# Tiles 2 and 3 of a grouped convolution in float32 by shared blocks and edges, with the turn of a tile issued last on VectorE

## The reference

```python
out = conv(x, weight, groups=4, taps=9, pad=4)          # x: (128, 32, 512)
y   = out + (c @ c_weight.T)[:, :, None] + bias[None, :, None]
base_out = y @ base_W.T + base_b                        # over the last axis, 512 -> 512
probs = softmax(y @ router_W.T + router_b)              # 15 routes
topk_p, topk_i = top_k(probs, 8)
w = sum over k of topk_p * onehot(expert_map[topk_i])   # 8 experts
lora = ((y @ A.T) * w) @ B * 2.0                        # 8 experts of rank 16
x + base_out + lora
```

## Time and profile before

| | us |
|---|---|
| median of 3 runs | 184.52 (184.43 to 621.96) |
| the profiled execution, its own time | 184.44 |
| its span in the profile | 182.6 |
| PE busy | 178.4 (98%), 1236 instructions |
| DVE, POOL, ACT busy | 150.8, 139.8, 81.2 |

### The profile page before, as it was taken

The page is one execution under the profiler, slowest core; times in us unless marked ns, Lnnn a source line. Parts: engine busy times, 40 slices in busy tenths (PEclk is TensorE's granted clock), DMA queues, the critical chain, the costliest instruction groups (busy, mean ns, idle before and its releaser), DMA issues.

```text
span 182.6 us, 3930 instructions
## 1 busy us (share of the span) xinstructions
PE 178.4 (98%) x1236; PEld 171.1 (94%) x1236; DVE 150.8 (83%) x509; ACT 81.2 (44%) x247; POOL 139.8 (77%) x139
## 2 busy tenths in 40 slices
PE   7999999999999999999999999999999999999993
PEld 3687999999999999999999999999999999999992
DVE  0597888898888889888888988889898889978673
ACT  3648743354544434454443445454344444422320
POOL 2118999999888898888889888888988887885620
PEclk9999999999999999999999999999999999999999
DMA  6999751757475553646565454656445721233304
GB/s 172 348 388 340 252 178 14 243 199 204 152 233 174 173 181 124 178 152 230 159 198 174 135 170 154 228 178 210 175 106 201 230 78 63 97 115 115 118 0 172
DMA packets 17876, 32.01 MB, mean 175 GB/s; under 512 B 1984, under 2 KB 3136, under 8 KB 17856
## 3 DMA queue, kind: packets, MB, share of 16 engines
q1 hardware_dynamic: 17424, 31.40, 53.1%
q10 hardware_dynamic: 432, 0.36, 0.6%
HBM read 23.36 MB, written 8.39 MB: 174 GB/s over the span
## 4 chain that ended last, share of the span: by engine, by line
PE 96%; DVE 2%; issue 0%; POOL 0%; DVEq 0%; POOLq 0%
PE wide_ps L606 62%; PE wide_ps L648 12%; PE conv_banks L592 11%; PE edge_bank L592 3%; PE conv_banks L606 2%; PE odd_bank L635 2%; PE wide_ps L554 2%; PE conv_banks L663 1%; PE conv_banks L565 1%; PE conv_banks L563 1%; DVE xr L966 1%; DVE y L856 0%; DVE y_rows L774 0%; PE edge_bank L621 0%; DVE y_hi L891 0%
## 5 line engine op out<-in xcount | busy, mean ns | idle before, releaser
L606 PE MATMUL wide_ps<-wide_hi,y_hi 128*128 128x400 f32 (+1 forms) x248 | 66.0, 326 | 0.1
L606 PE MATMUL wide_ps<-wide_hi,y_lo 128*128 128x400 f32 (+1 forms) x248 | 62.6, 313 | 0.0
L606 PE MATMUL wide_ps<-wide_lo,y_hi 128*128 128x400 f32 (+1 forms) x248 | 62.5, 313 | 0.0
L486 POOL TENSOR_TENSOR terms_lo<-terms,terms_hi 128x512 fp32r<-128x512 f32 x28 | 36.3, 1298 | 18.4 <-ACT terms_hi L385 18.4
L606 PEld LDWEIGHTS wide_ps<-wide_hi,y_hi 128*128 128x128 f32 x248 | 44.0, 188 | 2.5 <-issue 0.5
L606 PEld LDWEIGHTS wide_ps<-wide_lo,y_hi 128*128 128x128 f32 x248 | 45.9, 188 | 0.0
L606 PEld LDWEIGHTS wide_ps<-wide_hi,y_lo 128*128 128x128 f32 x248 | 45.9, 188 | 0.0
L504 POOL TENSOR_TENSOR y_lo<-y,y_hi 128x512 fp32r<-128x512 f32 x31 | 40.3, 1299 | 5.7 <-ACT y_hi L400 5.7
L481 POOL TENSOR_TENSOR xr<-xr,base_b_sb 128x512 f32<-128x512 f32 x32 | 41.7, 1302 | 0.0
L407 ACT ACTIVATE hw_hi<-odd_bank 128x128 fp32r<-128x128 f32 x31 | 8.6, 278 | 54.3 <-PE odd_bank L635 54.3
L768 DVE TENSOR_TENSOR xr<-wide_ps,xr 128x512 f32<-128x512 f32 x30 | 20.7, 691 | 5.2 <-PE wide_ps L648 3.8
(11 more groups left out here) (90 smaller groups left out, 308.4 us busy)
## 6 DMA issues: line engine op xcount, KB each, us to landing
xr<-x_rows SPq DMA_DIRECT2D x32, 256.0 KB, 3.6
out<-xr SPq DMA_DIRECT2D x31, 256.0 KB, 3.2
terms<-x_units SPq DMA_DIRECT2D x28, 256.0 KB, 2.9
edges<-x_edges SPq DMA_DIRECT2D x14, 256.0 KB, 3.1
wide_sb<-wide_w SPq DMA_DIRECT2D x4, 328.0 KB, 4.9
x_in<-x_first SPq DMA_DIRECT2D x3, 264.0 KB, 4.7
weights_sb<-conv_w SPq DMA_DIRECT2D x2, 192.0 KB, 5.3
x_in<-x_first SPq DMA_DIRECT2D x2, 132.0 KB, 2.8
```

Of the source, the lines that this page charges most:

```text
L486: nc.gpsimd.tensor_tensor(terms_lo[i % 2][:, :, :, :], terms[i][:, :, :, :], terms_hi[i % 2][:, :, :, :].bitcast(F32), ALU.subtract)\
L606: mm = nc.tensor.matmul(sums_of(t, k)[:, b, 0:columns[1] - columns[0]], a[k % 2][:, r, :], w[:, r, columns[0]:columns[1]], start=r == 0 an ...
```

## The change

Tiles 2 and 3 no longer load whole blocks into `x_in` but even and odd blocks apart (`first_terms`) and one tile of edges (`first_edges`). `conv_whole` multiplies them by the shared, own and edge weights in plain float32, 256 columns each: three products for tile 2, two for tile 3. The differences that they need are made by POOL (tile 2 and the edges) and by DVE (tile 3), from SBUF to SBUF. Two weight blocks less are loaded, the pieces are cut otherwise, and the piece with the shared sums and quarter (now piece 4) is loaded ahead of piece 3. ACT takes the conditions of groups 2 and 3 ahead of `conv_high(1)`. On DVE the third addition of a condition becomes a function of its own (`reach`), and in every step the order is: two additions of the condition, `hw_low`, `choose`, `best`, `reach`, `add_out`, `mark`, `difference`, `weigh`, and the turn at the end. ACT takes `hw_high` ahead of `y_high` up to step 29. On POOL `bias_rows(0)` stands ahead of `edge_low(2)`. PE's `conv` waits for the edge's bank only ahead of the edge's products. `last_steps` is unchanged.

```diff
@@ -47,19 +48,18 @@
-W_OWN, W_REACH = (1, 2, 5, 6), (0, 3, 4, 7)
-W_SUM, W_QUARTERS = (8, 9, 11, 12), (10, 13)
-W_ALL = 14
+W_OWN, W_REACH, W_SUM, W_QUARTERS = (1, 2, 4, 7), (0, 3), (9, 10, 5, 8), (11, 6)
+W_ALL = 12
 COND = N + C + GROUPS + 2 * ROUTES
 W_PIECES = (slice(COND, COND + 2 * P), slice(COND + 2 * P, COND + 4 * P),
-            slice(COND + 4 * P, COND + 8 * P), slice(COND + 8 * P, COND + 11 * P),
-            slice(COND + 11 * P, COND + 14 * P))
-S_OWN, S_SUM, S_QUARTERS, S_ALL = (0, 1, 5, 6), (2, 3, 7, 8), (4, 9), 10
-S_PIECES = ((slice(0, 2), slice(1, 3), (0, 1)), (slice(2, 5), slice(8, 11), (3,)),
-            (slice(5, 7), slice(5, 7), (2,)), (slice(7, 10), slice(11, 14), (4,)))
+            slice(COND + 4 * P, COND + 7 * P), slice(COND + 7 * P, COND + 9 * P),
+            slice(COND + 9 * P, COND + 12 * P))
+S_OWN, S_SUM, S_QUARTERS, S_ALL = (0, 1, 5, 8), (2, 3, 6, 9), (4, 7), 10
+S_PIECES = ((slice(0, 2), slice(1, 3), (0, 1)), (slice(2, 5), slice(9, 12), (4,)),
+            (slice(5, 8), slice(4, 7), (2,)), (slice(8, 10), slice(7, 9), (3,)))
 def build(nc, x_first, x_units, x_edges, x_rows, conv_w, wide_w, up_w, base_b, out):
...
@@ -101,11 +101,14 @@
-        x_in = [sb(f"x_in{i}", [P, Q, BLKI]) for i in range(START)]
+        x_in = [sb(f"x_in{i}", [P, Q, BLKI]) for i in range(FIRST)]
+        first_terms = [sb(f"first_terms{i}", [P, 2, Q, MK]) for i in range(START - FIRST)]
+        first_edges = sb("first_edges", [P, 2, Q, MK])
         terms = [sb(f"terms{i}", [P, 2, Q, MK]) for i in range(URING)]
...
@@ -281,10 +292,13 @@
             load_conv(2)
-            load_x(2)
+            load_first_terms(0)
             sync.wait_ge(wide_in[0], 16)
+            sync.dma_start(first_edges[:, :, :, :], x_edges[0]).then_inc(first_edges_in, 16)
+            load_conv(4)
+            sync.wait_ge(wide_in[1], 16)
             load_conv(3)
-            load_x(3)
+            load_first_terms(1)
             sync.wait_ge(wide_in[2], 16)
...
@@ -414,12 +427,12 @@
             bias_condition(range(1, 2), 2)
+            bias_condition(range(2, GROUPS), 3)
             conv_high(1)
...
             exponentials(0, 0)
-            bias_condition(range(2, GROUPS), 3)
             terms_high(START, 0)
...
@@ -431,11 +444,14 @@
                     return
-                if up_to_tile(t, TILES - 2):
+                if t == TILES - 2:
                     y_high(t + 1, k + 1)
...
                 hw_high(t - 1, k - 1)
+                if up_to_tile(t, TILES - 3):
+                    y_high(t + 1, k + 1)
                 if up_to_tile(t, TILES - 2):
...
@@ -512,6 +528,14 @@
             conv_low(0)
+            pool.wait_ge(first_terms_in[0], 16)
+            nc.gpsimd.tensor_tensor(first_terms[0][:, 0, :, :], first_terms[0][:, 0, :, :],
+                                    first_terms[0][:, 1, :, :], ALU.subtract)\
+                .then_inc(first_difference[0], 1)
+            pool.wait_ge(first_edges_in, 16)
+            nc.gpsimd.tensor_tensor(first_edges[:, 0, :, :], first_edges[:, 0, :, :],
+                                    first_edges[:, 1, :, :], ALU.subtract)\
+                .then_inc(first_edge_ready, 1)
             conv_low(1)
...
@@ -521,14 +545,14 @@
                     up_low()
-                    edge_low(p + 2, k // 2)
                     pool.wait_ge(base_b_in, 16)
                     bias_rows(t, k)
+                    edge_low(p + 2, k // 2)
                     y_low(t + 2, k + 2)
...
                 if t == 1:
+                    bias_rows(t, k)
                     terms_low(t + 4, k)
-                    bias_rows(t, k)
                     edge(p + 3, 1 - k // 2)
...
@@ -572,21 +596,15 @@
                          (conv_ps[:, h, 1, :, :], S_OWN[g], terms_hi[h][:, 0], terms_lo[h][:, 0])]
-                if t == START:
-                    pe.wait_ge(y_rows_ready, t - 1)
-                    pe.wait_ge(cond_biased, GROUPS)
-                elif h == 0:
-                    pe.wait_ge(y_rows_ready, t)
-                else:
-                    pe.wait_ge(y_rows_ready, t - 1)
+                pe.wait_ge(y_rows_ready, t - 1)
                 if h == 0:
...
                     if n == 2:
+                        pe.wait_ge(y_rows_ready, t)
                         pe.wait_ge(edge_lo_ready, p - START // 2 + 1)
...
@@ -669,11 +687,24 @@
             cond_sums(range(1, 2), 2)
-            def conv_later(t):
+            def conv_whole(t):
+                i, h = t - FIRST, t % 2
                 pe.wait_ge(y_rows_ready, t - 1)
-                pe.wait_ge(conv_w_in[2], 16)
-                pe.wait_ge(x_loaded[t], 16)
-                conv_first(t)
+                pe.wait_ge(conv_w_in[2 + i], 16)
+                pe.wait_ge(first_terms_in[i], 16)
+                nc.tensor.matmul(conv_ps[:, h, 0, :, :], conv_sb[:, W_SUM[t], :],
+                                 first_terms[i][:, 1, :, :], start=True, stop=True)
+                pe.wait_ge(first_difference[i], 1)
+                mm = nc.tensor.matmul(conv_ps[:, h, 1, :, :], conv_sb[:, W_OWN[t], :],
+                                      first_terms[i][:, 0, :, :], start=True, stop=True)
+                if h == 0:
+                    pe.wait_ge(cond_biased, GROUPS)
+                    pe.wait_ge(first_edge_ready, 1)
+                    mm = nc.tensor.matmul(edge_ps, conv_sb[:, W_QUARTERS[t // 2], :],
+                                          first_edges[:, 0, :, :], start=True, stop=True)
+                mm.then_inc(conv_done, 1)
             def first_step():
...
@@ -779,21 +810,26 @@
                 rows = y_rows[h]
-                reached = slice(EDGE, P) if h == 0 else slice(0, EDGE)
                 dve.wait_ge(conv_done, t + 1)
...
                     .then_inc(common_ready, 1)
-                dve.wait_ge(common_ready, t - START + 1)
+                dve.wait_ge(common_ready, t - FIRST + 1)
                 nc.vector.tensor_tensor(rows[:, :, other, :], conv_ps[:, h, 1, :, :],
                                         rows[:, :, shared, :], ALU.add).then_inc(own_ready, 1)
-                dve.wait_ge(own_ready, t - START + 1)
+            def reach(t, g):
+                h = g % 2
+                shared = 1 - h
+                rows = y_rows[h]
+                reached = slice(EDGE, P) if h == 0 else slice(0, EDGE)
+                dve.wait_ge(own_ready, t - FIRST + 1)
                 nc.vector.tensor_tensor(rows[reached, :, shared, :], edge_ps[reached],
...
@@ -898,36 +934,40 @@
             best(0, 0)
-            difference(START, 0)
             dve.wait_ge(top_ready, 1)
             mark(0, 0)
+            dve.wait_ge(first_terms_in[1], 16)
+            nc.vector.tensor_tensor(first_terms[1][:, 0, :, :], first_terms[1][:, 0, :, :],
+                                    first_terms[1][:, 1, :, :], ALU.subtract)\
+                .then_inc(first_difference[1], 1)
+            difference(START, 0)
             dve.wait_ge(is_expert_ready, 1)
...
                 if t == 0:
-                    condition_first(2)
+                    condition(2, 2, 0)
+                    reach(2, 2)
                     turn(2, 2)
+                    hw_low(0, 0)
                     choose(1, 1)
...
                     best(1, 1)
+                    condition(3, 3, 0)
+                    reach(3, 3)
+                    return
+                if t == 1:
+                    add_out(0, 0)
                     dve.wait_ge(top_ready, 2)
                     mark(1, 1)
-                    condition_first(3)
-                    hw_low(0, 0)
-                    return
-                if t == 1:
+                    difference(START + 1, 1)
+                    weigh(1, 1)
                     turn(3, 3)
-                    difference(START + 1, 1)
-                    add_out(0, 0)
-                    weigh(1, 1)
                     return
...
                     condition(t + 2, (k + 2) % GROUPS, q + (k + 2) // GROUPS)
-                    turn(t + 2, k + 2)
-                    hw_low(t - 1, k - 1)
-                elif t == TILES - 2:
+                if up_to_tile(t, TILES - 2):
                     hw_low(t - 1, k - 1)
...
@@ -943,17 +983,19 @@
                     return
-                if up_to_tile(t, TILES - 2):
-                    choose(t, k)
-                    dve.wait_ge(logits_ready, t + 1)
-                    if up_to_tile(t, TILES - 5):
-                        difference(t + 4, k)
-                    best(t, k)
-                    dve.wait_ge(top_ready, t + 1)
-                    if up_to_tile(t, TILES - 3):
-                        add_out(t - 1, (k - 1) % UNROLL)
-                    mark(t, k)
-                    weigh(t, k)
+                choose(t, k)
+                dve.wait_ge(logits_ready, t + 1)
+                best(t, k)
+                if up_to_tile(t, TILES - 3):
+                    reach(t + 2, (k + 2) % GROUPS)
+                    add_out(t - 1, (k - 1) % UNROLL)
```

(7 more changed lines are left out.)

29 lines of the change are left out of this document (18 added, 11 removed).

## The result

The changed kernel takes 186.88 us (median of 6 executions, 186.31 to 188.23) beside 184.83 us for the kernel before on the same chip: a ratio of 1.0126 with a 95% interval of 1.0076 to 1.0176, so 2.3 us slower (1.4 to 3.3). That is within 2%, as forecast, and slower by more than the 0.9 us forecast, outside the range of 184.5 to 186.3.

What follows compares the result with a forecast made beforehand. PE bounds the kernel, with 96% of the chain of waits. From a span of 182.6 us, less 0.6 at the start, 0 in the middle, plus 1.6 at the end, plus 1.8 around it: 185.4 us, range 184.5 to 186.3.

Steps and rivals of the forecast that it cites:

- Cost: none, with 1.4 us of cover: Start: POOL's two subtractions of 0.75 us fit where POOL stood idle, before PE asks for the edges; no cost.
- 0 us, 28 times over: Middle steps: the new order moves operations later, but covers of 0.75 to about 1 us absorb it; 0 us.
- Tail, +1.6: Last steps: the late turn of tile 31 delays `y_hi`, `y_lo` and PE's front bank; 1.6 us lost, bounds 1.4 to 1.8.
- The rival that hides it: Tail: idle time absorbs the last turn's delay, so only the start counts; 183.8 or 183.1 us, chance 0.08.
- gains 0.6 us: Start: 1.29 us of PE work removed, 0.4 given back waiting for `up_lo` and 0.2 for `edge_lo`; 0.6 us gained.
- the sense of the rival: Middle: PE's transpose waits for `odd_up` behind the later `difference`; 188.2 us and more, slower by over 2%, chance 0.04.
- The rival of DVE and POOL blocking each other: Start: POOL's subtractions and DVE's two-input SBUF operations wait for each other; 0.5 to 0.8 us on the sum, chance 0.25.
- the pair at 14 us: Start: DVE's subtraction for tile 3 beside POOL's `conv_lo`, colliding for 0.4 us of POOL's full queue if the engines block.
- The base: Whole kernel: counted from the profiled execution of 184.44 us, span 182.6 and 1.8 around it; median taken as 184.52.
- 1.29 us less work: Start, PE: tile 2's convolution costs 0.43 us less and tile 3's 0.86 less, 1.29 us of work removed.

Runs made afterwards that it cites:

- before_tail_late: Kernel before with only step 29 in the changed order (turn of tile 31 last, `y_high` behind `hw_high`): 186.78 us, 1.0094.
- after_4: Changed kernel run again unedited for one more trace; the traced execution took 186.64 us.
- after_3: Changed kernel run again unedited for one more trace; the traced execution took 187.37 us.
- after_2: Changed kernel run again unedited, a second set of 6 executions: 186.96 us, 1.0113; the traced execution took 187.90 us.
- after: First profiled execution of the changed kernel, unedited: 188.23 us, where that set's median is 186.88 us.
- no_up_lo: tail_mid with POOL's subtraction for the low part of the up weights left out, zeros in its place: 184.73 us, 1.0000.
- pool_reads: Kernel before plus two POOL subtractions, SBUF to a scratch tile, placed beside DVE's `wide_lo`: 186.06 us, 1.0054.
- sub_late: Changed kernel, but POOL's first subtractions wait until DVE has made all four `wide_lo`: 186.86 us, 1.0108.
- sub_late_2: sub_late run once more, on the same chip as after_2: 186.39 us, 1.0086.
- both_mended: Changed kernel with the edit of sub_late and step 29 in the old order on DVE and ACT: 185.54 us, 1.0028.
- tail_mid: Changed kernel with sub_late's edit; in step 29 DVE turns right behind `reach`, `add_out` goes last, ACT takes `y_high` ahead of `hw_high`: 185.17 us, 1.0028.
- old_middle: Changed kernel with sub_late's edit, and DVE and ACT in the old order from step 2 to the end: 185.71 us, 1.0045.
- no_subs: tail_mid with the three subtractions for tiles 2 and 3 replaced by one-element fills: 184.71 us, 0.9989.

## Why the prediction was wrong

Two terms that the prediction put at nothing cost time: POOL's two subtractions beside `wide_lo` ("Cost: none, with 1.4 us of cover"), which cost 0.3 to 1.2 us, and the middle ("0 us, 28 times over"), which cost 0.5.

- **Tail, +1.6.** Right: 1.58 to 1.60 in the four traces of the changed kernel, and 1.63 in `before_tail_late`, which has nothing else of the change. The path was the one written down. The rival that hides it is dead.
- **The start, "gains 0.6 us".** This step failed, by the collision. Its four pieces, by PE's starts (the forecast is worked out from the prediction's own terms):

  | us | before | forecast | after_4 | after_3 | after_2 | after |
  |---|---|---|---|---|---|---|
  | cond sums to the next products | 0.36 | 0.36 | 0.69 | 1.03 | 1.57 | 1.57 |
  | tile 2's convolution to tile 3's | 3.91 | 3.58 | 3.66 | 3.66 | 3.67 | 3.67 |
  | tile 3's to transpose 0 | 1.72 | 0.86 | 0.86 | 0.87 | 0.86 | 0.86 |
  | transposes 0 to 1 | 5.50 | 6.07 | 6.12 | 6.15 | 6.14 | 6.13 |

  Left out is the piece between the first two, 0.68 before and 0.70 or 0.71 after. The last three pieces are within 0.1 of the forecast each and give a gain of 0.4 to 0.5. `no_up_lo` shows that the wait between the transposes is `up_lo`'s, with `edge_lo` behind it. The first piece takes 0.33 of that back in `after_4`, and more than all of it (0.67 to 1.21) in the others. The prediction asked who would wait for POOL's subtractions, and was right that nobody does; it didn't put into the sum that they hold up DVE's `wide_lo`, for which PE waits. `pool_reads` shows that cause alone. With the edit of `sub_late` and the whole computation the start still takes 11.87 to 12.19 (`sub_late`, `sub_late_2`, `both_mended`, `tail_mid`, `old_middle`), a gain of 0 to 0.3, since there the collision at `y_lo` of tile 1 takes about 0.3.
- **The middle, "0 us, 28 times over".** This step failed: +0.46 to +0.56 in each of the four traces of the changed kernel. 0.14 of it is the one late start of `hw_hi` of tile 24, 0.3 the slower odd step; the cause of both stays open. No cover was gone in the sense of the rival: each distance is within 0.3 of before.
- **The rival of DVE and POOL blocking each other**, at 0.25, is what happens in every trace of the changed kernel, and I had priced it at 0.5 to 0.8 on the sum. It is 0.3, 0.7 or 1.2 by the execution. Of its two places only the first collides there; the pair at 14 us costs there 0.06 of DVE's time at most, and more only behind the edit of `sub_late`. Over both sets the changed kernel's 14 executions have a mean of 187.1, the 12 of `sub_late` one of 186.7: 0.4 on the mean, 0.2 on the median, what the collision costs less what that edit costs. I had weighed the rival by what the rows of before could show. They could show nothing, since in that trace DVE's two-input operations never met POOL at work. Where a change brings two engines together for the first time, that silence is no evidence against. In another execution of the old start they do meet: in `before_tail_late` `wide_lo` runs until 13.02, and `conv_lo` takes 1.44 instead of 0.86:

```profile
12.31 1.44 POOL L477 TENSOR_TENSOR conv_lo<-weights_sb,conv_hi 128x384 fp32r<-128x384 f32 x1 [4.03 <-ACT conv_hi L350]
```

- **The base.** I counted from the profiled execution of 184.44; over more executions on the chips used here the kernel before has medians of 184.73 to 184.91. That is 0.4 of the miss. The trace of that execution came to the cond sums at 11.87, earlier than all others here.

Together, as an estimate from these rows: 185.4, +0.4 for the base, +0.15 for the start without the collision, +0.5 for the middle and +0.3 to 1.2 for the collision give 186.8 to 187.7, beside medians of 186.9 and 187.0 measured.

## What to carry to other kernels

A subtraction of float32 with both inputs in SBUF on VectorE and one on GpSimd don't run side by side: put them where the other engine is idle, and if a load decides when they meet, look at several executions, since one trace shows one draw. PE work that is removed ahead of a full queue comes back as a wait on that queue: of 1.29 us less work 0 to 0.3 arrived in the start of the versions with the whole computation, and moving one operation within the queue only moved the wait. Mending one meeting of two engines by a delay can make the next: with POOL's subtractions behind `wide_lo`, it was `y_lo` that collided. When an order is changed for a loop, write out the last two or three steps on their own; one turn in its late place there cost more than all else.

## What the hardware showed unexpectedly

The blocking is fair, one for one: in the changed kernel's first trace, with both queues full, the two engines' ends alternate every 0.6 to 0.7 us, so each operation on either side lasts its own time and 0.5 to 0.6 of the other's (0.84 becomes 1.36 to 1.38, 0.75 becomes 1.32). The profile counts the waiting as part of the operation, with no idle time ahead of it; a longer mean is the only sign. Writes by POOL (memset of 128x256, 0.27 each) cost DVE nothing. And steps with the same instructions run at slightly different speed by what stands ahead of them: from step 2 on `pool_reads` is the kernel before, yet its odd steps take 5.11 or 5.12 from transpose 5 on (but for the pair 24, 25), without the turns of 5.11 and 5.15; `no_subs` is `tail_mid` there, and takes 5.12 where that takes 5.14 or 5.15. Why stays open, and each is one trace.
